# A fused cross-attention and mixture-of-experts kernel: TensorE does the shared chunk ahead of the attention work in steps 16 and later

## The chip, the cores and the metric

The kernel runs on one core of a Trainium2 chip. Its metric is the device time of one execution in microseconds (us). A core has five engines that run their own instruction streams and meet only at semaphores: TensorE (PE: matmuls and transposes), VectorE (DVE), ScalarE (ACT: activation functions and copies), GpSimd (POOL) and SyncE (SP: it issues DMA transfers). Each engine takes its instructions strictly in the order in which they are written, so an instruction that waits holds up all that stand behind it on its engine. PE writes its results to PSUM, from where ACT or DVE take them.

## What is computed

`x` has 4 x 512 rows of 256 numbers, `ctx` has 4 x 64 rows. In float32:

```python
x = x + attn(layernorm(x), ctx)          # 16 heads of 16, softmax over 64 context rows, output product Wo, bias bo
z = layernorm(x)                         # 2048 rows
sh = gelu(z @ sw1[s] + sb1[s])           # s = 0, 1: two shared experts, hidden width 512
shared = (sum_s sh @ sw2[s] + sb2[s]) / 2
gates = z @ router_w + router_b          # 8 experts, the best 2 of each row, softmax over the two
moe = sum over the two chosen experts e of p_e * (gelu(z @ w1[e] + b1[e]) @ w2[e] + b2[e])
out = x + shared + moe
```

## The kernel before

The 2048 rows are 16 tiles of 128 (`NT = 16`). A first part runs attention tile by tile, a second the shared experts, a third the routed experts over rows gathered by expert. Products of the second and third part are split into a high and a low part (`s_hi`, `s_lo`, `xt_hi`, `xt_lo`, `h_hi`, `h_lo`) and summed from three matmuls each.

The first two parts are one pipeline over steps `s = 0 .. 47`, written out on every engine as a loop `for s in range(FIRST_CHUNK + CHUNKS)` with `FIRST_CHUNK = 16` and `CHUNKS = 32`. What a step holds is fixed by hand. On PE (L1146 to L1242), in this order:

- `scores(s + 1)` while there are tiles;
- the **attention part** of the step, four pieces that belong to four tiles: transposes of the normalised rows of tile s - 8 (L1154, `psA<-ident,rows`; two tiles in step 22), the output product of tile s - 4 (L1165, `psD<-WoT,OT`), the values product of tile s - 3 (L1177, `psA<-PT,Vbd`), and the eight transposes of the probabilities of tile s - 2 (L1190, `psP<-ident,Pr`). In steps 16 to 22 this pipeline drains: the last probabilities are transposed in step 17, the last values product is in step 18, the last output product in step 19, the last rows in step 22;
- `queries`, in odd steps up to 11;
- from step 16 on the **shared chunk** `n = s - 16`: in chunk 1 first `gate_rows_out(0)` (L1106, `psS<-ident,gT`), from chunk 2 on `shared_out(n - 2)` (12 matmuls, L1122 and L1125), then six matmuls of the hidden layer (L1215, `psS<-xt_hi,s_lo` and so on);
- after it, in some steps, router work: `gate_cols(0)` in step 16 and `gate_cols(1)` in step 23 (L1098), and the ranking matmuls in steps 19 and 26 (L1237, L1239).

ACT's step (L590 to L648) is not touched: copy of the transposed rows out of psA (L595), copy of the values product into `OT` (L602), normalised rows of tile s - 7 (L610), copy of the transposed probabilities psP into `PT` (L616), and behind these, from step 16 on, the two Gelus of chunk n (L632 into `h_hi`, L633 into `g`). In step 16 a table load (L622) stands ahead of the Gelus, since all activations before it used other functions, and the copy of the gate columns (L637, `gT<-psS`) behind them. DVE's step: residual add of tile s - 4 (L906, `xres<-psD,xres`), statistics, then `h_lo` of chunk n (L929). Behind `h_lo` stand in step 17 `choose(0)` (L785 and L789: it reads the gate rows from PSUM and signals `gates_read`), in step 18 `indices(0)` and `one_hot(0)` (L796 to L808, `ohs`), in step 20 `place(0)`.

Waits of PE that the prediction speaks of: chunk 0 waits for `xlo_done` (DVE L765); `gate_rows_out(0)` waits for `gt_sb` (ACT L637); `shared_out(0)` waits, since it writes the banks from which probabilities and gate rows are read, for `pt_sb` of the last tile (ACT L616) and `gates_read` (DVE L785); the ranking in step 19 waits for `ohs_ready` (DVE L808) and for `x1_done` of the last tile (DVE L906). Later, DVE L982 waits for scatter-adds of POOL, which begin when all results of the shared experts are stored (POOL L502).

Of the kernel before, what the change touches and what calls it, by code (L numbers as in the profile page):

```python
# [17 lines left out]
NT = TOK // P  # L18
# [12 lines left out]
NPAIR = NT // 2  # L31
# [6 lines left out]
CHUNKS = NG * NSH * HC  # L38
CPG = NSH * HC
FIRST_CHUNK = NT  # L40
# [72 lines left out]
def program(nc, ios, keep, scratch):  # L113
# [4 lines left out]
    with ExitStack() as es:  # L118
# [3 lines left out]
        def sem(name):  # L122
            return es.enter_context(nc.semaphore(name))
# [63 lines left out]
        xbo_done, x1_done, x1s_done, sbh_done = sem("xbo_done"), sem("x1_done"), sem("x1s_done"), sem("sbh_done")  # L187
# [33 lines left out]
        def x2T_at(s):  # L221

            return range(s - 8, NT) if s == NT + 6 else range(max(s - 8, 0), s - 7) if s < NT + 6 else ()
# [18 lines left out]
        def row(t):  # L242

            return rows[t // HALF_T][:, t % HALF_T]
# [790 lines left out]
        def _(pe):  # L1035
# [13 lines left out]
            def queries(p):  # L1049
                if p == 1:  # L1050
                    pe.wait_ge(ld_xT0, 16)
                elif p % 2 == 0:
                    pe.wait_ge(ld_xT[2 * p // TPB], 16)
                pe.wait_ge(qt_sb, p)
                for f in range(C):
                    for c in range(C):
                        last = T.matmul(psD[:, f * D:(f + 1) * D], WqT[:, c, f * P:(f + 1) * P], xTs[:, c, p * QT_TOK:(p + 1) * QT_TOK],
                                        start=(c == 0), stop=(c == C - 1))
                last.then_inc(qt_psum, 1)

            def scores(t):
                b = t // TPB
                pe.wait_ge(qt_sb, t // 2 + 1)
                if b == 0:
                    pe.wait_ge(k0_done, 1)
                else:
                    pe.wait_ge(k_done, HPR)
                if t >= 2:
                    pe.wait_ge(shift_done, t - 1)
                for c in range(C):  # L1070
                    for r in range(RT):
                        own = slice(r * L, (r + 1) * L)
                        last = T.matmul(psS[:, t % 2, r, c * HPR * L:(c + 1) * HPR * L], QT[own, t // 2 % 2, c, t % 2 * P:(t % 2 + 1) * P],  # L1073
                                        Kbd[own, c, b].rearrange("p h k -> p (h k)"), start=True, stop=True)
                last.then_inc(scores_done, 1)
# [26 lines left out]
            def gate_rows_out(h):  # L1102

                pe.wait_ge(gt_sb, h + 1)
                for i in range(HALF_G):
                    last = T.transpose(gate_rows[h][:, i * P:(i + 1) * P], gT[:, HALF_G * h + i], ident[:])  # L1106
                last.then_inc(gates_psum, 1)
# [35 lines left out]
                        last = T.transpose(xt_bank[s % 2][:, first:first + P], xg[:, b + u, c * P:(c + 1) * P], ident[:])  # L1143
                last.then_inc(xt_psum, 1)

            for s in range(FIRST_CHUNK + CHUNKS):  # L1146
                if s + 1 < NT:
                    scores(s + 1)
                for t in x2T_at(s):
                    pe.wait_ge(rows_done, t + 1)  # L1150
                    pe.wait_ge(ot_sb, min(s - 3, NT))
                    first = (t - x2T_at(s)[0]) * D
                    for c in range(C):
                        last = T.transpose(psA[:, first + c * P:first + (c + 1) * P], row(t)[:, c * P:(c + 1) * P], ident[:])  # L1154
                    last.then_inc(x2t_psum, 1)
                if 4 <= s < NT + 4:
                    t = s - 4
                    if t == 0:
                        pe.wait_ge(ld_wo, 16)
                    pe.wait_ge(ot_sb, t + 1)  # L1160
                    pe.wait_ge(qt_sb, min(s // 2 + 2, NPAIR))
                    if t >= 1:
                        pe.wait_ge(x1_done, t)
                    for c in range(C):
                        last = T.matmul(psD[:, 0:D], OT[:, t % 2, c], WoT[:, c], start=(c == 0), stop=(c == C - 1))  # L1165
                    last.then_inc(att_psum, 1)
                if 3 <= s < NT + 3:
                    t = s - 3
                    pe.wait_ge(pt_sb, t + 1)
                    if t == 0:  # L1170
                        pe.wait_ge(v_done, 4)
                    if t >= 5:
                        pe.wait_ge(x2t_sb, t - 4)
                    for c in range(C):
                        for j in range(TPB):
                            own = slice(CT * j, CT * (j + 1))
                            last = T.matmul(psA[own, D + c * P:D + (c + 1) * P], Vbd[:, t // TPB, c * P + CT * j:c * P + CT * (j + 1)],  # L1177
                                            PT[:, t % 2, 4 * (j // 2) + 2 * c + j % 2], start=True, stop=True)
                    last.then_inc(ot_psum, 1)
                if 2 <= s < NT + 2:  # L1180
                    t = s - 2
                    pe.wait_ge(probs_done, t + 1)
                    if t == 0:
                        pe.wait_ge(consts, 2)
                        pe.wait_ge(v_done, 4)
                        pe.wait_ge(k_done, HPR)
                    else:
                        pe.wait_ge(pt_sb, t)
                    for j in range(NJ):
                        last = T.transpose(psP[:, j // 4, j % 4 * P:(j % 4 + 1) * P], Pr[:, t % NPR, 2 * j:2 * j + 2].rearrange("p h k -> p (h k)"), ident[:])  # L1190
                    last.then_inc(pt_psum, 1)
                if s % 2 == 1 and 2 <= (s + 3) // 2 < NPAIR:
                    if s >= 4:
                        pe.wait_ge(x1_done, s - 3)
                    queries((s + 3) // 2)

                n = s - FIRST_CHUNK
                if n == 1:
                    gate_rows_out(0)
                if 0 <= n - 2 < CHUNKS - 2:  # L1200
                    shared_out(n - 2)
                if 0 <= n < CHUNKS:
                    q, e, k = n // CPG, n % CPG // HC, n % HC
                    if n == 0:
                        pe.wait_ge(shift_done, NT - 1)
                        pe.wait_ge(s_lo_done, NSH * PPE)
                    if n % CPG == 0:
                        pe.wait_ge(xlo_done, q + 1)
                    if n >= 2:
                        pe.wait_ge(g_done, n - 1)  # L1210
                    i = 0
                    for c in range(C):
                        wc = slice(c * HF + k * P, c * HF + (k + 1) * P)
                        for a, b in ((s_lo, xt_hi), (s_hi, xt_lo), (s_hi, xt_hi)):
                            last = T.matmul(h_bank[n % 2], a[:, e, wc], b[:, q % 2, c], start=(i == 0), stop=(i == 3 * C - 1))  # L1215
                            i += 1
                    last.then_inc(h_psum, 1)
                if n == 0:
                    pe.wait_ge(ld_small, 16 * 4)
                    pe.wait_ge(shift_done, NT)  # L1220
                    gate_cols(0)
                if n == 7:
                    pe.wait_ge(x1_done, NT)
                    pe.wait_ge(slots_ready, 1)
                    gate_cols(1)
                if n == 8:
                    gate_rows_out(1)
                if n in (3, 10):
                    h = n // 10
                    pe.wait_ge(ohs_ready, h + 1)  # L1230
                    pe.wait_ge(consts, 24)
                    if h == 0:
                        pe.wait_ge(x1_done, NT)
                    end = HALF_T if h == 0 else NT + 1
                    for t in range((h + 1) * HALF_T):
                        first = max(t, h * HALF_T)
                        T.matmul(psD[:, first * NE:end * NE].rearrange("p (t e) -> p t e", e=NE), ones[:],  # L1237
                                 ohs[:, t].unsqueeze(1).to_broadcast([P, end - first, NE]), start=(t == 0), stop=False)
                    T.matmul(psD[:, h * HALF_T * NE:(h + 1) * HALF_T * NE], tri[:], ohs[:, h * HALF_T:(h + 1) * HALF_T].rearrange("p t e -> p (t e)"),  # L1239
                             start=False, stop=True).then_inc(ranks_psum, 1)  # L1240
                if CHUNKS - 3 <= n < CHUNKS - 1:
                    x_transpose(n - CHUNKS + 3)  # L1242
# [41 lines left out]
            for t in range(SLOTS + 1):  # L1284
# [26 lines left out]
                if 1 <= t <= SINGLES:  # L1311
                    n = t - 1
# [8 lines left out]
                if 2 <= t < SINGLES + 2:  # L1321
                    n = t - 2
# [129 lines left out]
```

## Time and profile before

| | us |
|---|---|
| median of 3 runs | 349.05 |
| lowest and highest | 346.09, 352.20 |
| the profiled execution | 349.37 |
| its span, first to last instruction | 347.7 |

| engine | busy us | share of the span |
|---|---|---|
| PE | 313.0 | 90% |
| DVE | 227.3 | 65% |
| ACT | 216.8 | 62% |
| POOL | 193.4 | 56% |

Busy time of PE is of matmuls that overlap, and their ends are modelled: the time from one start to the next tells what one takes, and the last of a group seems to run on beside the first of the next. The mean granted TensorE clock is 0.972 of full speed. Steps 16 to 23 lie at about 95 to 131 us in this execution.

### The profile page before, as it was taken

To read this page: it belongs to the slowest core of one execution; us is meant where nothing else is said; L and a number is where in the kernel's file an instruction comes from. 1 tells how busy PE (TensorE), PEld (TensorE's weight loads), DVE (VectorE), ACT (ScalarE), POOL (GpSimd) and SP (SyncE) were. 2 spreads that over 40 slices of the span, in tenths; PEclk is the share of its full clock that TensorE was granted. 3 is DMA by queue.
4 is the path that set the end of the run, shared out by engine and by line. 5 is a ranking of instruction groups with operands and counts; after the bars stand their busy time and mean duration, and the time that the engine had idled before them with its cause. 6 is when DMAs were issued, how large, how long until landed. Compare 5 with 4: busy or idle time off the path is not lost. (4 is left out here: it accounts for less than half of the span.)

```text
span 347.7 us, 7628 instructions
## 1 busy us (share of the span) xinstructions
PE 313.0 (90%) x2366; PEld 273.2 (79%) x2366; DVE 227.3 (65%) x474; ACT 216.8 (62%) x437; POOL 193.4 (56%) x235
## 2 busy tenths in 40 slices
PE   3996998999689999998999999999699999999980
PEld 2764776676467878897898998999599999999980
DVE  0579897898943567787566455667557767666630
ACT  1253675876775786574556656677277777868640
POOL 5446899879893268776460000333456557456563
PEclk9996999999999999999899999999899999999996
DMA  7980000007100472346666523545436557534344
GB/s 248 407 333 2 1 2 1 2 0 270 35 16 3 141 268 79 137 139 178 183 221 182 132 111 105 91 69 93 61 54 86 92 79 109 83 38 50 46 45 45
DMA packets 27910, 36.85 MB, mean 106 GB/s; under 512 B 8384, under 2 KB 22080, under 8 KB 27488
## 3 DMA queue, kind: packets, MB, share of 16 engines
q1 hardware_dynamic: 19984, 25.02, 23.6%
q0 software_dynamic: 7456, 10.04, 17.1%
q10 hardware_dynamic: 432, 1.31, 1.1%
q8 instruction: 20, 0.33, 0.4%
q14 instruction: 18, 0.15, 0.2%
HBM read 23.17 MB, written 13.19 MB: 105 GB/s over the span
## 5 line engine op out<-in xcount | busy, mean ns | idle before, releaser
L508 POOL DMA_INDIRECT out<-xres,meta x39 | 65.1, 1669 | 43.0 <-DMA out<-xres,meta 21.4
L929 DVE TENSOR_TENSOR h_lo<-g,h_hi 128x512 fp32r<-128x512 f32 x32 | 23.3, 728 | 39.8 <-ACT g L633 36.5
L632 ACT ACTIVATE h_hi<-psS,sb1T 128x512 fp32r<-128x512 f32 x32 | 22.0, 688 | 34.5 <-PE psS L1215 30.4
L471 POOL TENSOR_TENSOR Pr<-Pr,inv 128x1024 f32<-128x1024 f32 x16 | 31.3, 1958 | 12.0 <-DVE inv L918 11.9
L718 ACT ACTIVATE s_hi<-psS,b1c 128x256 fp32r<-128x256 f32 x60 | 25.6, 490 | 19.6 <-PE psS L1260 19.6
L1276 PE MATMUL psP<-w_lo,s_hi 128*128 x120 | 30.2, 284 | 3.3 <-DVE xres L982 3.3
L1026 DVE TENSOR_TENSOR s_lo<-sraw,s_hi 128x512 fp32r<-128x512 f32 x30 | 20.6, 688 | 18.7 <-ACT sraw L721 14.8
L1276 PE MATMUL psP<-w_hi,s_hi 128*128 x120 | 30.1, 282 | 0.0
L1215 PE MATMUL psS<-xt_hi,s_lo 128*128 128x512 f32 x64 | 25.9, 405 | 0.0
L721 ACT ACTIVATE sraw<-psS,b1c 128x256 f32<-128x256 f32 x60 | 25.9, 503 | 0.0
L1215 PE MATMUL psS<-xt_lo,s_hi 128*128 128x512 f32 x64 | 25.7, 402 | 0.0
L1276 PEld LDWEIGHTS psP<-w_lo,s_hi 128*128 128x128 f32 x120 | 22.8, 190 | 3.5 <-DVE xres L982 3.5
L1215 PE MATMUL psS<-xt_hi,s_hi 128*128 128x512 f32 x64 | 25.4, 397 | 0.0
L1190 PE MATMUL psP<-ident,Pr 128*128 128x128 f32 x128 | 18.7, 292 | 6.2 <-POOL Pr L471 6.1
L1276 PEld LDWEIGHTS psP<-w_hi,s_hi 128*128 128x128 f32 x120 | 23.0, 192 | 0.0
L1190 PEld LDWEIGHTS psP<-ident,Pr 128*128 128x128 f32 x128 | 14.7, 148 | 10.1 <-POOL Pr L471 8.5
L441 POOL DMA_INDIRECT xg_d<-rows_a,slots x16 | 18.3, 1142 | 7.4 <-issue 4.0
L778 DVE TENSOR_TENSOR w_lo<-wraw,w_hi 128x512 fp32r<-128x512 f32 x32 | 21.9, 714 | 0.0
L633 ACT ACTIVATE g<-psS,sb1T 128x512 f32<-128x512 f32 x32 | 21.8, 682 | 0.0
L441 POOL DMA_INDIRECT xg_d<-rows_b,slots x16 | 18.2, 1137 | 5.3 <-issue 5.1
L886 DVE TENSOR_REDUCE mx<-psS 128x16 f32<-128x1024 f32 x16 | 18.7, 1169 | 3.6 <-PE psS L1073 3.6
L607 ACT ACTIVATE Pr<-Pr,rs 128x1024 f32<-128x1024 f32 x16 | 18.3, 1144 | 4.4 <-DVE Pr L895 4.4
(238 smaller groups left out, 1013.8 us busy)
## 6 DMA issues: line engine op xcount, KB each, us to landing
wraw<-in_w SPq DMA_DIRECT2D x16, 512.0 KB, 5.1
xg<-xg_d SPq DMA_DIRECT2D x15, 256.0 KB
sraw<-in_sw SPq DMA_DIRECT2D x2, 1024.0 KB, 11.3
out<-xres SPq DMA_DIRECT2D x4, 512.0 KB
xres<-in_x SPq DMA_DIRECT2D x3, 512.0 KB, 9.3
xTs<-in_xT SPq DMA_DIRECT2D x3, 512.0 KB, 10.0
xg<-xg_d SPq DMA_DIRECT2D x9, 128.0 KB
xg_d<-filler SPq DMA_DIRECT2D x8, 130.0 KB
```

The costliest lines, as they stand in the source:

```text
L441: pool.indirect_dma_start(xg_d, bass.IndirectOffsetOnAxis(ap=slots[:, k, t:t + 1], axis=0), row(t), None).then_inc(scattered[t // HALF_T][ ...
L471: pool.tensor_tensor(out=Pr[:, t % NPR], in0=Pr[:, t % NPR], in1=inv[:, t % 2].unsqueeze(2).to_broadcast([P, NH, L]), op=ALU.mult).then_in ...
L508: pool.indirect_dma_start(out, bass.IndirectOffsetOnAxis(ap=meta[:, n, 0:1].bitcast(U32), axis=0), y[:, n % NYB], None, compute_op=ALU.add ...
L632: A.activation(h_hi[:, n % 2], h_bank[n % 2], ACT.Gelu, bias=bias).then_inc(hhi_done, 1)
L633: A.activation(g[:, n % 2], h_bank[n % 2], ACT.Gelu, bias=bias).then_inc(g_done, 1)
L718: ins = A.activation(hp_hi[:, i % 2, k], hp_bank[i % 2][k], ACT.Gelu, bias=b1c[:, i % 2, k:k + 1])
L721: ins = A.activation(gp[:, i % 2, k], hp_bank[i % 2][k], ACT.Gelu, bias=b1c[:, i % 2, k:k + 1])
L778: V.tensor_tensor(out=w_cols(w_lo[:, e], k), in0=w_cols(wraw[e], k), in1=w_cols(w_hi[:, e], k).bitcast(F32), op=ALU.subtract).then_inc(lo_ ...
L929: V.tensor_tensor(out=h_lo[:, n % 2], in0=g[:, n % 2], in1=h_hi[:, n % 2].bitcast(F32), op=ALU.subtract).then_inc(hlo_done, 1)
L1190: last = T.transpose(psP[:, j // 4, j % 4 * P:(j % 4 + 1) * P], Pr[:, t % NPR, 2 * j:2 * j + 2].rearrange("p h k -> p (h k)"), ident[:])
L1215: last = T.matmul(h_bank[n % 2], a[:, e, wc], b[:, q % 2, c], start=(i == 0), stop=(i == 3 * C - 1))
L1276: T.matmul(res_bank[n % 2], hp_hi[:, i % 2, c, own], b[:, bass.ds(e, 1), C * HF + c * D:C * HF + (c + 1) * D].squeeze(1), start=(c == 0 an ...
```

## The change

The attention part of a step and the shared chunk become functions, `attention(s)` and `chunk(n)`. Up to step 15 nothing changes. From step 16 on PE does `chunk(s - 16)` first and `attention(s)` after it. No instruction is added or removed, and DVE, ACT, POOL and SP keep their order.

```diff
--- before.py
+++ after.py
@@ -1143,9 +1143,7 @@
                         last = T.transpose(xt_bank[s % 2][:, first:first + P], xg[:, b + u, c * P:(c + 1) * P], ident[:])
                 last.then_inc(xt_psum, 1)
 
-            for s in range(FIRST_CHUNK + CHUNKS):
-                if s + 1 < NT:
-                    scores(s + 1)
+            def attention(s):
                 for t in x2T_at(s):
                     pe.wait_ge(rows_done, t + 1)
                     pe.wait_ge(ot_sb, min(s - 3, NT))
@@ -1189,12 +1187,8 @@
                     for j in range(NJ):
                         last = T.transpose(psP[:, j // 4, j % 4 * P:(j % 4 + 1) * P], Pr[:, t % NPR, 2 * j:2 * j + 2].rearrange("p h k -> p (h k)"), ident[:])
                     last.then_inc(pt_psum, 1)
-                if s % 2 == 1 and 2 <= (s + 3) // 2 < NPAIR:
-                    if s >= 4:
-                        pe.wait_ge(x1_done, s - 3)
-                    queries((s + 3) // 2)
-
-                n = s - FIRST_CHUNK
+
+            def chunk(n):
                 if n == 1:
                     gate_rows_out(0)
                 if 0 <= n - 2 < CHUNKS - 2:
@@ -1215,6 +1209,21 @@
                             last = T.matmul(h_bank[n % 2], a[:, e, wc], b[:, q % 2, c], start=(i == 0), stop=(i == 3 * C - 1))
                             i += 1
                     last.then_inc(h_psum, 1)
+
+            for s in range(FIRST_CHUNK + CHUNKS):
+                if s + 1 < NT:
+                    scores(s + 1)
+                if s < NT:
+                    attention(s)
+                if s % 2 == 1 and 2 <= (s + 3) // 2 < NPAIR:
+                    if s >= 4:
+                        pe.wait_ge(x1_done, s - 3)
+                    queries((s + 3) // 2)
+
+                n = s - FIRST_CHUNK
+                if n >= 0:
+                    chunk(n)
+                    attention(s)
                 if n == 0:
                     pe.wait_ge(ld_small, 16 * 4)
                     pe.wait_ge(shift_done, NT)
```

In the lists below a row is a group of equal matmuls of PE in program order; line numbers are those of each kernel (L1209, L1188, L1175, L1163, L1152 in the changed one are L1215, L1190, L1177, L1165, L1154 before). The first place is the end of step 16 and the start of step 17. Before:

```order
L1215 MATMUL psS<-xt_hi,s_hi 128x512
L1098 MATMUL psS<-x2T_a,rws 32x128 x16
L1154 MATMUL psA<-ident,rows_b 128x128 x2
L1165 MATMUL psD<-WoT,OT 128x256 x2
L1177 MATMUL psA<-PT,Vbd 32x128 x8
L1190 MATMUL psP<-ident,Pr 128x128 x8
L1106 MATMUL psS<-ident,gT 128x128 x2
L1215 MATMUL psS<-xt_hi,s_lo 128x512
L1215 MATMUL psS<-xt_lo,s_hi 128x512
L1215 MATMUL psS<-xt_hi,s_hi 128x512
```

After the change:

```order
L1152 MATMUL psA<-ident,rows_b 128x128 x2
L1163 MATMUL psD<-WoT,OT 128x256 x2
L1175 MATMUL psA<-PT,Vbd 32x128 x8
L1188 MATMUL psP<-ident,Pr 128x128 x8
L1098 MATMUL psS<-x2T_a,rws 32x128 x16
L1106 MATMUL psS<-ident,gT 128x128 x2
L1209 MATMUL psS<-xt_hi,s_lo 128x512
L1209 MATMUL psS<-xt_lo,s_hi 128x512
L1209 MATMUL psS<-xt_hi,s_hi 128x512
L1209 MATMUL psS<-xt_hi,s_lo 128x512
```

`gate_rows_out(0)` (L1106) and the first hidden matmuls of chunk 1 now follow directly on `gate_cols(0)` (L1098). The four attention groups that stood between them have moved behind chunk 1.

The second place is the end of step 17 and the start of step 18, up to the first matmul of `shared_out(0)` (L1122). Before:

```order
L1215 MATMUL psS<-xt_hi,s_hi 128x512
L1154 MATMUL psA<-ident,rows_b 128x128 x2
L1165 MATMUL psD<-WoT,OT 128x256 x2
L1177 MATMUL psA<-PT,Vbd 32x128 x8
L1122 MATMUL psS<-s_lo,h_hi 128x256
```

After the change:

```order
L1209 MATMUL psS<-xt_hi,s_hi 128x512
L1152 MATMUL psA<-ident,rows_b 128x128 x2
L1163 MATMUL psD<-WoT,OT 128x256 x2
L1175 MATMUL psA<-PT,Vbd 32x128 x8
L1188 MATMUL psP<-ident,Pr 128x128 x8
L1122 MATMUL psS<-s_lo,h_hi 128x256
```

Between the end of chunk 1 and `shared_out(0)` stood three groups of step 18; now the four groups of step 17 stand there, and the last of them is the transposes of the last probabilities. Those of step 18 follow behind chunk 2. In steps 19 to 22 the same exchange is made with the rest of the attention part.

## Rows read from the trace of the kernel before

**Rows 1.** Busy us per engine in a stretch; at the end TensorE clock, DMA share, GB/s.
```profile
101.00:106.00 5.00, 4.21 (x52) 3.25 (x41) 2.39 (x4) 4.01 (x9) 2.73 (x3) 1.00 0.08 26
...
124.00:130.00 6.00, 6.00 (x42) 5.21 (x46) 4.08 (x6) 4.80 (x9) 5.20 (x5) 1.00 0.64 236
```

**Rows 2.** Timeline of PE, step 16: start, length, engine, line, operation [idle before].
```profile
95.76 0.44 PE L1154 MATMUL psA<-ident,rows_b 128*128 128x128 f32 x2 [1.00 <-ACT rows_b L610]
...
98.71 0.47 PE L1215 MATMUL psS<-xt_hi,s_lo 128*128 128x512 f32 x1
...
100.27 1.08 PE L1098 MATMUL psS<-x2T_a,rws 128*32 128x128 f32 x32
...
101.28 0.44 PE L1154 MATMUL psA<-ident,rows_b 128*128 128x128 f32 x2
```

**Rows 3.** Timelines of DVE (first row) and ACT (the rest), steps 15 and 16.
```profile
94.89 1.16 DVE L765 TENSOR_TENSOR xt_lo<-x2T_a,xt_hi 128x1024 fp32r<-128x1024 f32 x1
...
98.99 1.03 ACT L616 ACTIVATE PT<-psP 128x1024 f32<-128x1024 f32 x1 [0.38 <-PE psP L1190]
...
100.03 1.28 ACT L622 ACT_TABLE_LOAD   x1
...
102.58 0.38 ACT L637 ACTIVATE gT<-psS 128x256 f32<-128x256 f32 x1
```

**Rows 4.** Timeline of PE, steps 17 and 18.
```profile
103.38 0.65 PE L1177 MATMUL psA<-PT,Vbd 128*32 128x128 f32 x16 [0.79 <-ACT x2T_b L595]
...
103.95 1.09 PE L1190 MATMUL psP<-ident,Pr 128*128 128x128 f32 x8
...
104.88 0.38 PE L1106 MATMUL psS<-ident,gT 128*128 128x128 f32 x2
...
109.09 0.36 PE L1122 MATMUL psS<-s_lo,h_hi 128*128 128x256 f32 x1
...
111.98 0.38 PE L1154 MATMUL psA<-ident,rows_b 128*128 128x128 f32 x2
```

**Rows 5.** Timelines of ACT (first two rows) and DVE (last two), step 17.
```profile
105.08 1.03 ACT L616 ACTIVATE PT<-psP 128x1024 f32<-128x1024 f32 x1
...
106.71 0.69 ACT L632 ACTIVATE h_hi<-psS,sb1T 128x512 fp32r<-128x512 f32 x1 [0.60 <-PE psS L1215]
...
108.00 0.69 DVE L929 TENSOR_TENSOR h_lo<-g,h_hi 128x512 fp32r<-128x512 f32 x1 [2.86 <-ACT g L633]
...
108.61 0.22 DVE L785 TENSOR_TENSOR gates<-psS,rb_bc 128x64 f32<-128x64 f32 x1
```

**Rows 6.** Timelines of ACT (two rows), DVE (two), PE (two), steps 18 to 23.
```profile
109.09 0.39 ACT L602 ACTIVATE OT<-psA 128x256 f32<-128x256 f32 x1 [0.84 <-PE psA L1177]
...
109.37 0.59 ACT L610 ACTIVATE rows_b<-xres,nmr,rs 128x256 f32<-128x256 f32 x1
...
113.48 0.69 DVE L929 TENSOR_TENSOR h_lo<-g,h_hi 128x512 fp32r<-128x512 f32 x1 [2.97 <-ACT g L633]
...
116.24 0.39 DVE L906 TENSOR_TENSOR xres<-psD,xres 128x256 f32<-128x256 f32 x1
...
116.77 0.35 PE L1237 MATMUL psD<-ohs,ones 128*128 128x64 bf16 x8 [0.72 <-DVE xres L906]
...
129.90 1.08 PE L1098 MATMUL psD<-x2T_b,rws 128*32 128x128 f32 x32
```

**Rows 7.** PE after its longest idle times, and the stretches around the last two.
```profile
28.91 1.97 PE L1190 MATMUL psP<-ident,Pr 128*128 128x128 f32 x8 [3.70 <-POOL Pr L471]
...
163.32 0.35 PE L1122 MATMUL psS<-s_lo,h_hi 128*128 128x256 f32 x1 [1.67 <-issue]
...
249.36 0.39 PE L1276 MATMUL psP<-w_lo,s_hi 128*128 x1 [3.29 <-DVE xres L982]
...
160.00:170.00 10.00, 8.33 (x42) 7.03 (x41) 5.13 (x10) 4.11 (x7) 2.94 (x5) 0.83 0.80 231
...
240.00:260.00 20.00, 16.71 (x126) 16.32 (x125) 10.79 (x19) 11.76 (x32) 8.56 (x7) 0.91 0.38 58
```

## The prediction

> **What bounds the kernel now.** I read the stretches first. From 124 us on PE is busy without a break and the clock is full; in 101 to 106 us it is busy for 4.21 of 5 us only [rows 1]. So PE sets the pace, and in steps 16 to 19 it stands still at times for others. What moves the end of these steps moves everything behind them: the shared chunks that follow keep PE full. Next I read PE's timeline there for what it waits on. In step 16 it is idle 1.00 us for the rows [rows 2]. In step 17 it is idle 0.79 us for ACT's copy of the rows [rows 4], in step 19 0.72 us for DVE's L906 [rows 6]. `gate_rows_out(0)` at 104.88 does not wait: the gate columns it needs left ACT at 102.58 + 0.38 = 102.96 [rows 3]. `shared_out(0)` at 109.09 hardly waits: DVE's L785 ends at 108.61 + 0.22 = 108.83 [rows 5]. Both points were covered by attention work of PE, and this is what the change takes away.
>
> **The change, part by part.** No work is added; what counts is who waits for whom. Lengths of PE's pieces, from start to start: an attention part of step 17 is 104.88 - 101.28 = 3.60 us, less 0.79 of idle time and some 0.2 by which the last modelled matmul outlasts its place: 2.6 us, of which the transposes of probabilities take 104.88 - 103.95 = 0.93 [rows 2, 4]. `gate_cols(0)` is 101.28 - 100.27 = 1.0 [rows 2]. `shared_out` and the six hidden matmuls are 111.98 - 109.09 = 2.9 together [rows 4], the hidden ones alone 1.5 (98.71 to 100.27) [rows 2]; in chunk 1 there are the two gate transposes beside them, 1.6. From the end of a DVE instruction to PE's start I count 0.14 us (116.24 + 0.39 to 116.77) [rows 6].
>
> *Step 16.* Chunk 0 must wait for `xt_lo`, which DVE has at 94.89 + 1.16 = 96.05 [rows 3]: it starts at 96.2, later than the rows allowed before (95.76). It is done at 97.7, the attention part at 100.3, `gate_cols(0)` at 101.3: as before. But the transposes of tile 14's probabilities end at 100.4 instead of 98.95, so ACT's copy of them starts at 100.5 instead of 98.99, and behind it on ACT stand the table load, both Gelus and the gate columns [rows 3]. All of these move by 1.5. The gate columns are there at 102.96 + 1.5 + 0.14 = 104.6. PE comes to `gate_rows_out(0)` at 101.3 already, since the attention part of step 17 stands behind it now. **First wait: 3.3 us.**
>
> *Step 17.* Gate rows and chunk 1 run from 104.6 to 106.2, much as before; the attention part from 106.2 to 108.8, and its last transpose ends at 109.0. ACT copies these probabilities at 109.0 (105.08 before). The Gelus of chunk 1 stand behind that copy, at 109.9; before they waited for the chunk until 106.71. `h_lo` comes 108.00 - 106.71 = 1.3 later, the gates 0.6 after that and take 0.2 [rows 5]: 112.1. With 0.14 `shared_out(0)` starts at 112.2 instead of 109.09. PE had finished at 108.8. **Second wait: 3.4 us.**
>
> *Steps 18 and 19.* `shared_out(0)` and chunk 2 take 2.9, the attention part without probabilities 2.6 - 0.93 = 1.7: the last values product is done at 116.8. Behind it on ACT: the copy into `OT` at 116.9, the rows 0.3 later, the Gelus 0.5 after that [rows 6], `h_lo` 1.3 later at 119.0. Then DVE's index work in its old length, from `h_lo` to L906 116.24 - 113.48 = 2.8, and 0.5 from there to the ranking matmuls [rows 6]: 122.2 instead of 116.77, 5.5 late. PE's own work ends at 116.8 + 2.9 + 1.1 = 120.7. **Third wait: 1.5 us.**
>
> *Steps 20 to 23.* `shared_out(n)` of chunk n + 2 needs Gelus that are two steps old. ACT now does rows and copies of a step after the chunk's matmuls, so that the Gelus come about 1.4 later after their chunk, and a step has 2.9 us of shared work: hidden. The rows wait for nothing any more, which gives back some 0.3. `gate_cols(1)`, at 129.90 before [rows 6], comes at 135.1: **+5.2 us**. The weights' transfers start when DVE's L906 is through with the last tile, and move with it; POOL's and SP's work hangs on results that move too. I give nothing back for them.
>
> *The clock.* After idle times of 1.67 and 3.29 us PE's clock fell to 1.2 GHz for a while. The stretches around them show 0.83 over 10 us and 0.91 over 20 us, so 1.7 and 1.8 us lost; after 3.70 us idle the eight transposes took 1.97 [rows 7] against 1.09 [rows 4]. Idle times of 0.79 to 1.00 left the clock at 1.00 [rows 1, 2]. The first new wait of 3.3 us belongs to the first kind, and every matmul from it to the second wait lies on the path: 1.7. So does the second, but what is slow after 116.8 is covered by the third wait: 1.1. Bounds: nothing, if the clock doesn't fall; and at the upper end all 4.2 and 4.6 us of work behind the two waits at half speed, 8.8. I take 2.8, since both measured falls cost less than 2.
>
> Sum: 349.4 + 5.2 + 2.8 = 357.4 against the profiled execution. That one is 0.3 above the median of the runs shown, so **357.0 us**, 2.3% more.
>
> One price on this path is disputed. ACT's table load takes 1.28 us [rows 3], and what stands ahead of it ends at 98.99 + 1.03 = 100.02, just before it starts at 100.03. The Trainium skill (ScalarE: Activation LUTs, What ACT_TABLE_LOAD costs) adds a drain of 1.38 us to each switch of the table set, 2.66 us in all. By that the first wait would be 4.7 and the sum 358.8; the trace shows no such gap here, and I stay with its row.
>
> **The rivals.**
> - *The clock stays full.* For it: each wait lies between stretches of full work, and the fall after 1.67 us idle came only later, with PE busy again. Against it: all three idle times over 1.6 us have slow matmuls behind them [rows 7]. Then 5.2 alone: 354.3 us. Chance 0.24.
> - *The clock stays low over most of the stretch between the waits.* For it: the 1.97 us after 3.70 us idle, and that here two long waits follow each other within 5 us, which the trace has nowhere. It costs 5 instead of 2.8, some 359.5 us. Chance 0.14.
> - *A later wait takes the loss up.* PE is idle for 3.29 us at 249.36 for DVE's L982 [rows 7], with 1.8 lost by the clock. If what ends that wait didn't move, 8.0 - 3.3 - 1.8 leave 2.9: 352 us. Against it: L982 waits for scatter-adds, and their first waits for the stores of all shared results, which are late by the same amount. Chance 0.05.
> - *Faster.* The idle times of 1.00, 0.79 and 0.72 us in PE [rows 2, 4, 6] go, since rows and copies are ready when PE comes to them, and with nothing else that gives 349.0 - 2.5 = 346.5 us. It is decided at `gate_rows_out(0)`: the gate columns would have to leave ACT by 101.2 us, but in the old order already they leave it at 102.96 [rows 3], and the change can only delay them. Chance 0.03.
> - My forecast, both waits and a fall of the clock behind them: the remaining 0.54.
>
> **How the numbers follow.** About 2% can be told from no change here; 2% over 349.05 is 356.0 us. The forecast's own range is 355.5 to 359, about 0.06 of its 0.54 below 356. So slower: 0.48 + 0.14 = 0.62; within 2%: 0.24 + 0.05 + 0.06 = 0.35; faster: 0.03. The range runs from 353.0, just under a clock that stays full, to 361.0, into the case in which it stays low; outside are the two lowest cases and the end of the highest.
>
> **What the profile would show.** PE idle about 3.3 us before L1106, its releaser ACT's gate columns, which leave ACT about 1.5 us later after chunk 0's start than the old order would have them; idle about 3.4 us before the first L1122, released by DVE's gates; about 1.5 us before L1237. Stretches behind the first two with a clock below 1.00. `gate_cols(1)` 5 to 8 us later than at 129.90, and from there to the end the same 218 us. The prediction is wrong if the first two waits are below 2 us, if the clock stays at 1.00 (then 354), or if the idle time ahead of the first scattered results (249.36 now) has shrunk.

## The result and the profile after

| | before | changed |
|---|---|---|
| median (lowest, highest) of 6 runs, us | 348.15 (346.09, 356.03) | 354.66 (352.08, 355.77) |
| ratio, 95% interval | | 1.0192 (1.0150 to 1.0234) |
| profiled execution, us (span) | 349.37 (347.7) | 352.16 (350.4) |
| medians of both again, beside each other on one chip (section on e9; 23 and 6 runs) | 345.04 | 354.44 |
| ratio there, 95% interval | | 1.0256 (1.0221 to 1.0292) |

The changed kernel is slower by 1.9% in the first measurement, whose interval holds 2%, and by 2.6% in the second, whose interval lies above it. The forecast was 357.0 us, 2.3%. Executions more than 1.5% above the fastest of their kernel (352.20 and 356.03 us of the kernel before here, 367.11 in e6) count as slow, and the ratios are made of the others.

PE of the changed kernel, steps 16 to 23 (timeline: start, length, engine, line, operation, idle time before and its releaser; L1209 and L1246 were L1215 and L1237):

```profile
94.71 0.47 PE L1209 MATMUL psS<-xt_hi,s_lo 128*128 128x512 f32 x1 [1.43 <-DVE xt_lo L765]
...
98.94 1.08 PE L1098 MATMUL psS<-x2T_a,rws 128*32 128x128 f32 x32
103.07 0.44 PE L1106 MATMUL psS<-ident,gT 128*128 128x128 f32 x2 [3.05 <-ACT gT L637]
...
110.91 0.36 PE L1122 MATMUL psS<-s_lo,h_hi 128*128 128x256 f32 x1 [3.33 <-DVE gates L785]
...
122.60 0.35 PE L1246 MATMUL psD<-ohs,ones 128*128 128x64 bf16 x8 [1.32 <-DVE xres L906]
...
135.15 1.08 PE L1098 MATMUL psD<-x2T_b,rws 128*32 128x128 f32 x32
```

ACT in steps 16 and 17, then DVE in step 17:

```profile
99.05 1.02 ACT L616 ACTIVATE PT<-psP 128x1024 f32<-128x1024 f32 x1
100.09 1.28 ACT L622 ACT_TABLE_LOAD   x1
...
102.63 0.38 ACT L637 ACTIVATE gT<-psS 128x256 f32<-128x256 f32 x1
...
107.61 1.02 ACT L616 ACTIVATE PT<-psP 128x1024 f32<-128x1024 f32 x1
108.53 0.68 ACT L632 ACTIVATE h_hi<-psS,sb1T 128x512 fp32r<-128x512 f32 x1
```

```profile
109.83 0.69 DVE L929 TENSOR_TENSOR h_lo<-g,h_hi 128x512 fp32r<-128x512 f32 x1 [2.92 <-ACT g L633]
110.44 0.22 DVE L785 TENSOR_TENSOR gates<-psS,rb_bc 128x64 f32<-128x64 f32 x1
```

The stretches of the changed kernel (busy us of PE, PEld, DVE, ACT, POOL; then the clock):

```profile
106.00:112.00 6.00, 2.67 (x32) 2.26 (x33) 2.51 (x13) 3.05 (x5) 0.35 (x2) 0.98 0.02 4
112.00:118.00 6.00, 6.00 (x41) 4.83 (x40) 0.85 (x2) 1.14 (x3) 2.28 (x4) 0.74 0.00 0
...
160.00:170.00 10.00, 9.67 (x61) 8.43 (x60) 9.20 (x27) 5.35 (x9) 8.73 (x5) 1.00 0.53 144
```

Against [rows 2, 4, 6] three idle times stand out: 3.05 us before the gate rows, 3.33 before the first `shared_out`, 1.32 before the ranking. The first is ended by ACT's copy `gT`, which stands behind the copy of the probabilities (99.05), the table load (100.09) and two Gelus. The second is ended by DVE's gates (110.44), behind `h_lo` (109.83), behind Gelus that begin only when ACT has copied the last probabilities (107.61 to 108.53). In 106 to 112 us PE is busy for 2.67 of 6 us. The clock, still at 0.98 there, is at 0.74 in the stretch behind the second wait.

All times below are counted from PE's transposes of tile 13's probabilities, in step 15, since this point itself lay anywhere between 91.5 and 94.1 us in the traces, whatever the kernel. The **local stretch** runs from there to `gate_cols(1)` in step 23: 129.90 - 93.67 = 36.23 us before, 135.15 - 92.19 = 42.96 after.

| from tile 13's transposes, us | before | changed | later by |
|---|---|---|---|
| `gate_cols(0)` | 6.60 | 6.75 | 0.15 |
| gate rows, L1106 | 11.21 | 10.88 | -0.33 |
| first `shared_out`, L1122 | 15.42 | 18.72 | 3.30 |
| ranking, L1237 | 23.10 | 30.41 | 7.31 |
| `gate_cols(1)` | 36.23 | 42.96 | 6.73 |

So the stretch is 6.7 us longer, yet the two profiled executions differ by 2.8 us only. Of the rest, 1.5 us is the earlier point in time of tile 13, and some 2.3 us lie in the kernel before (69.60 against 67.26 us in the section on e1): its first trace had the stall at 163.32 with the clock's fall behind it [rows 7], and the changed kernel's clock was at 1.00 through 160 to 170 us. Whether the change had removed that stall was the first thing to settle.

### The profile page after: what moved, and what is told of

It is laid out like the page before. It is cut to its first block and busy times, and to the rows that moved or that the text cites. A ratio compares the mean times of both kernels' runs of the same rounds, so it can differ in the third digit from the quotient of the medians.

```text
span 350.4 us, 7628 instructions
## 1 busy us (share of the span) xinstructions
PE 311.8 (89%) x2366; PEld 272.7 (78%) x2366; DVE 226.3 (65%) x474; ACT 216.8 (62%) x437; POOL 199.0 (57%) x235
## 3 DMA queue, kind: packets, MB, share of 16 engines
q10 hardware_dynamic: 432, 1.31, 1.1%
## 5 line engine op out<-in xcount | busy, mean ns | idle before, releaser
L929 DVE TENSOR_TENSOR h_lo<-g,h_hi 128x512 fp32r<-128x512 f32 x32 | 23.6, 737 | 36.2 <-ACT g L633 31.6
L1209 PE MATMUL psS<-xt_hi,s_lo 128*128 128x512 f32 x64 | 25.9, 405 | 1.4 <-DVE xt_lo L765 1.4
L1209 PE MATMUL psS<-xt_lo,s_hi 128*128 128x512 f32 x64 | 25.7, 402 | 0.0
L1209 PE MATMUL psS<-xt_hi,s_hi 128*128 128x512 f32 x64 | 25.3, 395 | 0.0
L441 POOL DMA_INDIRECT xg_d<-rows_b,slots x16 | 22.2, 1389 | 5.3 <-issue 5.1
L1188 PE MATMUL psP<-ident,Pr 128*128 128x128 f32 x128 | 18.5, 290 | 6.0 <-POOL Pr L471 5.9
L1188 PEld LDWEIGHTS psP<-ident,Pr 128*128 128x128 f32 x128 | 14.6, 147 | 9.8 <-POOL Pr L471 8.1
L1122 PE MATMUL psS<-s_lo,h_hi 128*128 128x256 f32 x64 | 17.8, 300 | 4.4 <-DVE gates L785 3.3
```

What stands on the lines that cost most here:

```text
L441: pool.indirect_dma_start(xg_d, bass.IndirectOffsetOnAxis(ap=slots[:, k, t:t + 1], axis=0), row(t), None).then_inc(scattered[t // HALF_T][ ...
L929: V.tensor_tensor(out=h_lo[:, n % 2], in0=g[:, n % 2], in1=h_hi[:, n % 2].bitcast(F32), op=ALU.subtract).then_inc(hlo_done, 1)
```

## The experiments

### e1: the kernel before, again

No edit.

> The kernel before, once more, to see what its trace repeats. I measure the local stretch on PE from the transposes of tile 13's probabilities (93.67 in the first trace) to gate_cols(1) (129.90): 36.2 us, and expect 36.0 to 36.5 again. Open is the rest of the span: the first trace had an idle time of 1.67 us of PE at 163 us with a fall of the clock behind it (some 3.4 us in all), which the changed kernel's trace does not have. If this belongs to the kernel before, it stands here too, and the change gives it back; if it comes and goes from run to run, the spans and clocks of the single runs spread by 2 to 4 us.

Measured: 345.56 us against 345.05 for the same kernel (ratio 1.0016, interval 0.9998 to 1.0034). The stretch is 36.23 us again, and each point of the table above agrees within 0.01. Where the stall was (columns as above):

```profile
160.00:165.00 5.00, 5.00 (x33) 4.59 (x34) 2.53 (x6) 2.70 (x5) 2.54 (x3) 1.00 0.86 170
```

PE is busy throughout at full clock. From `gate_cols(1)` to the weight load of the first transposes of gathered rows, 66.71 us pass here, 69.60 in the first trace of before, and 67.26 in the changed kernel's. The stall at 163 us is thus an accident of that execution and not a cost that the change takes away.

### e2, e3, e4: one part of the exchange at a time

The order in the loop is chosen by the step:

```diff
                 if n >= 0:
-                    chunk(n)
-                    attention(s)
+                    if s == 16:                # e3: s == 17, e4: s >= 18
+                        chunk(n)
+                        attention(s)
+                    else:
+                        attention(s)
+                        chunk(n)
```

> Chunk first in step 16 alone, the old order from step 17 on. Theory (the chain through ACT): the gate columns leave ACT 1.5 us late, and so does the copy of tile 9's rows behind them, for which the values product of step 17 waits; its idle time grows from 0.79 to 2.3 us, and the stretch becomes 36.2 + 1.5 = 37.7. Rival (each exchange costs the wait that was seen at its place): 3.1 to 3.3 more, 39.4. Clock stays at 1.00 in the stretch.

> Chunk first in step 17 alone. Theory: PE waits 1.8 us for the gate columns (they leave ACT at their old time), does the transposes of the last probabilities 2.6 us later, ACT's Gelus of chunk 1 move to behind their copy, and the first shared_out starts 1.6 us late; stretch 37.8. Rival (the wait of 3.4 us in front of shared_out belongs to this step alone): 39.6.

> Old order in steps 16 and 17, chunk first from step 18 on. Theory: shared_out(0) waits some 2.4 us for the gates, since it comes when chunk 1 is done and not after three attention groups; the last values product is 2.3 us late and with it the ranking; steps 19 to 22 cost nothing; stretch 36.2 + 2.0 = 38.2. Together with 1.5 and 1.6 of the other two parts this makes 5.1 of the 5.2 us forecast for the whole. Rival (the exchanges from 19 on cost or gain too): a stretch outside 37.7 to 38.7.

| | stretch, us | ratio (interval) |
|---|---|---|
| e2, step 16 only | 37.76 | 1.0085 (1.0051 to 1.0119) |
| e3, step 17 only | 38.00 | 1.0055 (1.0030 to 1.0079) |
| e4, from step 18 | 39.66 | 1.0133 (1.0101 to 1.0165) |

PE's idle times, of e2, e3 and e4 in this order:

```profile
103.63 0.65 PE L1175 MATMUL psA<-PT,Vbd 128*32 128x128 f32 x16 [2.18 <-ACT x2T_b L595]
```

```profile
102.44 0.44 PE L1106 MATMUL psS<-ident,gT 128*128 128x128 f32 x2 [1.65 <-ACT gT L637]
...
109.58 0.64 PE L1175 MATMUL psA<-PT,Vbd 128*32 128x128 f32 x16 [1.37 <-ACT x2T_b L595]
```

```profile
107.73 0.36 PE L1122 MATMUL psS<-s_lo,h_hi 128*128 128x256 f32 x1 [2.42 <-DVE gates L785]
```

e2 and e3 came out as forecast (37.7 and 37.8), and against the rivals at 39.4 and 39.6. The exchange in step 16 costs 1.5 us, of which 1.4 is the wait for ACT's rows, grown from 0.79 to 2.18; that in step 17 costs 1.8. By its medians e2 is 2.5 us longer than the kernel before beside it (347.56 against 345.05), more than its stretch explains; in its trace another 1.0 us lies behind the wait near 250 us, which the end of the part on why the prediction was right takes up. In e4 the stretch is 1.5 us over the forecast of 38.2. Its wait of 2.42 before `shared_out` is the one forecast (2.4). The difference is the clock:

```profile
108.00:110.00 2.00, 2.00 (x13) 2.00 (x13) 0.34 (x4) 0.00 (x0) 1.39 (x5) 0.63 0.04 8
110.00:112.00 2.00, 2.00 (x6) 1.52 (x6) 0.00 (x0) 0.00 (x0) 1.23 (x2) 0.52 0.00 0
```

It falls behind that wait, to 0.63 and 0.52 in four us: 2 x 0.37 + 2 x 0.48 = 1.7 us of PE's work. Without it e4 has 38.0. The three parts make 1.5 + 1.8 + 1.7 = 5.0 us without the clock, against 5.2 forecast for the whole.

### e12: chunk first from step 19 on

As above with `s >= 19`.

> Old order up to step 18, chunk first from step 19 on. Theory (the exchange in steps 19 to 22 costs nothing, since Gelus are needed two steps later and rows are ready): the ranking starts at its old time within 0.3 us, the stretch is 36.0 to 36.3, no fall of the clock, ratio 1.000. Rival (it is part of the loss): 37 or more.

Measured: stretch 35.49, below the 36.0 to 36.3 expected; ratio 1.0005 (0.9986 to 1.0023). PE's timeline at the ranking of step 19:

```profile
116.93 0.35 PE L1250 MATMUL psD<-ohs,ones 128*128 128x64 bf16 x8 [0.72 <-DVE xres L906]
```

From `gate_cols(0)` to the ranking e12 takes 116.93 - 100.44 = 16.49 us, as e1 does. From the ranking to `gate_cols(1)`, at 129.49, it takes 12.56 instead of 129.90 - 116.77 = 13.13 [rows 6]: the exchange in steps 20 to 22 gains 0.57 us. (The rest of the difference in the stretch, 0.16, lies before step 17: here, and in e11, the clock fell already around the start of the stretch, behind idle times of 1.00 and 0.92 us, and the transposes of tile 13 took 1.97 us instead of 1.09.) Its timeline at tile 13:

```profile
92.99 1.08 PE L1175 MATMUL psA<-PT,Vbd 128*32 128x128 f32 x16 [0.92 <-ACT x2T_a L595]
94.00 1.97 PE L1188 MATMUL psP<-ident,Pr 128*128 128x128 f32 x8
```

The gain doesn't show in the time. The waits of PE behind the stretch, of e1 first and of e12 below it, say why (engine, line, waited for: total, times, longest):

```profile
PE psD L1237 <- DVE ohs L808: 0.4, 1, 0.4
```

```profile
PE psD L1250 <- DVE ohs L808: 0.9, 1, 0.9
```

PE now comes earlier to the second ranking, in step 26, and waits for DVE 0.9 instead of 0.4 us there. The whole gain goes there.

### e9: the changed kernel, again

No edit.

> The changed kernel once more, beside the kernel before on the same chip. The waits of the stretch should repeat to 0.1 us (first L1106 10.9 and first L1122 18.7 us after tile 13's transposes); what should vary is where the clock falls: one fall in the first trace. The stretch is 43.0 with one fall, 44 to 45.5 with two or a long one, 41.4 with none. From gate_cols(1) to the first transposes of gathered rows I expect 66.7 to 67.3 us as in five traces so far, not the 69.6 of the very first one of the kernel before; then the ratio is 1.022, a little above the first measurement.

Measured: ratio 1.0256 (1.0221 to 1.0292), above the 1.022 expected. The waits are 3.05, 3.33 and 1.31 us, the gate rows stand at 10.90 (10.88 before), and the stretch is 44.36. Its clock, in two-us stretches behind either wait:

```profile
106.00:108.00 2.00, 2.00 (x6) 1.44 (x5) 0.00 (x0) 0.00 (x0) 0.00 (x0) 0.50 0.00 0
...
116.00:118.00 2.00, 2.00 (x7) 1.69 (x7) 0.00 (x0) 0.00 (x0) 1.63 (x4) 0.50 0.00 0
```

Here the clock fell behind both waits. The first fall delays the first `shared_out` from 18.72 to 20.12, by 1.4 us. The waits of the first trace and of this one are the same, so the same 3.05 us of idle time let the clock fall in one execution and not in the other.

### e5 and e10: PE kept busy in its waits

```diff
                 n = s - FIRST_CHUNK
+                if n in (1, 2):
+                    pe.wait_ge(x1_done, s - 4)
+                    for _ in range(26):        # e10: 13
+                        T.matmul(psD[:, D:D + P], ident[:], ident[:], start=True, stop=True)
                 if n >= 0:
                     chunk(n)
```

The added wait keeps PE out of the bank while DVE reads it; PE shows no idle time at it.

> The changed kernel with 26 matmuls of the identity with itself, whose result nobody reads, in each of its two long waits (ahead of the gate rows in step 17 and ahead of the first shared_out in step 18): 26 x 0.117 = 3.0 us of PE work each. Theory (part of the loss is the clock that falls behind the waits): PE's idle times there shrink to some 0.3 us, the clock stays at 1.00 up to 120 us, the local stretch is 36.2 + 5.2 = 41.4 instead of the 43.0 of the changed kernel's trace, and the runs lie 1 to 2.5 us below the changed kernel's, at a ratio of about 1.013 to before. Rival (the waits alone are the loss, the clock is of no account): the ratio stays at 1.019.

I had mis-sized the filler: the profile shows two records for each float32 matmul, so one takes 0.23 us and not 0.117. The 26 took 5.9 us at each place instead of 3.0, and the kernel's ratio is 1.0581 (1.0544 to 1.0618). The stretch is 46.42, the clock 1.00 all through it. Against the filler of the right size below, the gate rows come 13.70 - 10.91 = 2.79 us too late and the first `shared_out` 23.71 - 18.75 = 4.96, and that is the whole difference to 41.42. As a test of the time it failed. It lost another 10 us behind the stretch, where ACT waits for something whose releaser the profile gives as remote, no engine of the core (ACT's waits of 139 to 220 us; total, times, longest):

```profile
ACT h_hi L632 <- remote: 11.9, 3, 6.4
```

With the right size:

> The changed kernel with 13 instead of 26 filling matmuls of 0.23 us in each of the two long waits, 3.0 us of work each, whose result nobody reads. Theory (part of the loss is the clock): idle times of PE of 0.1 to 0.4 us at both places, clock 1.00 through the stretch, stretch 41.4 to 41.6 instead of 43.0, and runs 1 to 3 us below those of the changed kernel. Rival (clock of no account): stretch 43 and the same time. Whether the 10 us that the version with 26 lost between 150 and 180 us come back is open; if they do, they belong to the longer program of PE and not to the lateness.

Measured: stretch 41.42 us, and 352.70 us where e9, beside it on the same chip, has 354.44; ratio 1.0207 (1.0181 to 1.0233). PE at the first `shared_out`, and the clock behind the two places:

```profile
112.40 0.36 PE L1122 MATMUL psS<-s_lo,h_hi 128*128 128x256 f32 x1 [0.43 <-DVE gates L785]
```

```profile
104.00:106.00 2.00, 2.00 (x14) 1.65 (x13) 0.79 (x2) 0.50 (x2) 0.33 (x1) 1.00 0.00 0
...
114.00:116.00 2.00, 2.00 (x12) 1.64 (x11) 0.00 (x0) 0.30 (x1) 1.82 (x4) 1.00 0.00 0
```

The idle times are 0 and 0.43, the clock doesn't fall, and the gate rows stand at 10.91, the first `shared_out` at 18.75 as in the changed kernel's first trace. This parts the two causes. The waits alone make 41.42 - 36.23 = 5.19 us. The clock makes 1.5 us more in the first trace of the changed kernel, 2.9 in e9, and 1.7 between the medians of e9 and e10 (354.44 and 352.70; their runs overlap only at the edge, 352.56 to 356.83 and 350.93 to 352.99). The 10 us that e5 lost behind the stretch are gone too; since both fillers lengthen the program, and e10's by half as much, I can't say whether length or lateness brought them.

### e6: ACT takes the chunk first too

ACT's two Gelus, with the table load ahead of them, move in front of the copies of the attention part:

```diff
-                for t in x2T_at(s):
...
+                if s == NT:
+                    A.activation(warm[:], half[:], ACT.Gelu)
...
+                    A.activation(h_hi[:, n % 2], h_bank[n % 2], ACT.Gelu, bias=bias).then_inc(hhi_done, 1)
+                    A.activation(g[:, n % 2], h_bank[n % 2], ACT.Gelu, bias=bias).then_inc(g_done, 1)
+                for t in x2T_at(s):
...
-                if s == NT:
-                    A.activation(warm[:], half[:], ACT.Gelu)
...
-                    A.activation(h_hi[:, n % 2], h_bank[n % 2], ACT.Gelu, bias=bias).then_inc(hhi_done, 1)
-                    A.activation(g[:, n % 2], h_bank[n % 2], ACT.Gelu, bias=bias).then_inc(g_done, 1)
```

> The changed kernel with ACT's order exchanged too from step 16 on: the Gelus of the chunk first, then the copies of the attention part, and the copy of the gate columns after them. Theory (the loss comes from ACT's copies standing ahead of its Gelus while PE has them the other way round): both long waits shrink, the first to 0.7, the second to 1.3 us, the ranking starts at its old time, and the stretch is 36.2 again within 0.5. Rival (PE's order alone makes the loss, whatever ACT does): above 40.

Measured: stretch 38.34, ratio 1.0043 (1.0008 to 1.0079). PE's waits:

```profile
95.29 0.47 PE L1210 MATMUL psS<-xt_hi,s_lo 128*128 128x512 f32 x1 [1.45 <-DVE xt_lo L766]
...
98.78 0.64 PE L1176 MATMUL psA<-PT,Vbd 128*32 128x128 f32 x16 [0.78 <-ACT x2T_b L608]
...
101.97 0.44 PE L1107 MATMUL psS<-ident,gT 128*128 128x128 f32 x2 [0.51 <-ACT gT L638]
...
105.50 0.65 PE L1176 MATMUL psA<-PT,Vbd 128*32 128x128 f32 x16 [0.64 <-ACT x2T_b L608]
...
108.38 0.36 PE L1123 MATMUL psS<-s_lo,h_hi 128*128 128x256 f32 x1 [1.21 <-ACT PT L629]
```

The two long waits are 0.51 and 1.21 us as forecast (0.7 and 1.3), so the clash of the two orders is what makes them. But I expected 36.2 and missed by 2.1 us. The rows of the attention part now wait behind Gelus on ACT, and the values products of steps 16, 17 and 18 wait for them, 0.78, 0.64 and 0.64 us (the last at 113.16). With the wait ahead of chunk 0, which the exchange on PE brings, these are 1.45 + 0.78 + 0.51 + 0.64 + 1.21 + 0.64 = 5.2 us of idle time up to the ranking. The old order has 1.00 and 0.79 [rows 2, 4] and two more of 0.18 and 0.64, 2.6 in all. The difference of 2.6 is the ranking's delay, 25.77 against 23.10. The clock is 1.00 all through. So of the 5.2 us by which the changed kernel's stretch is longer without the clock, 3.1 go when ACT's order goes with PE's, and 2.1 remain with the exchange on both engines.

### e7, e8, e11: the table load where ACT idles

```diff
+                if s == NT:
+                    A.activation(warm[:], half[:], ACT.Gelu)
                 if 3 <= s < NT + 3:
                     t = s - 3
                     act.wait_ge(ot_psum, t + 1)
...
                 if s == NT:
-                    A.activation(warm[:], half[:], ACT.Gelu)
                     act.wait_ge(ld_small, 16 * 4)
```

> The changed kernel with ACT's table load for Gelu moved ahead of the copy into OT in step 16, where ACT idles. Theory: the load of 1.28 us leaves the path to the gate columns; the first wait is 1.9 us instead of 3.1 and the stretch, without the clock, 41.4 - 1.3 = 40.1. Rival (a drain of 1.38 us belongs to the switch and lies on the path too): the first wait is shorter by 2.6.

In the changed kernel the wait for the gate rows shrinks from 3.05 to 1.62, by 1.43; the gate rows come 1.41 us earlier. That is the load of 1.28 us and 0.1 of `warm` behind it. ACT at the load, and the clock around the end of PE's second wait (at 109.15), three of the five stretches below full:

```profile
96.25 0.38 ACT L595 ACTIVATE x2T_b<-psA 128x256 f32<-128x256 f32 x1 [1.47 <-PE psA L1153]
96.66 1.28 ACT L598 ACT_TABLE_LOAD   x1
```

```profile
108.00:110.00 2.00, 0.85 (x4) 0.88 (x5) 1.65 (x11) 0.04 (x1) 0.13 (x1) 0.50 0.02 4
...
112.00:114.00 2.00, 2.00 (x7) 1.52 (x6) 0.00 (x0) 0.00 (x0) 0.66 (x1) 0.50 0.00 0
114.00:116.00 2.00, 2.00 (x17) 1.41 (x18) 0.14 (x1) 0.38 (x1) 0.00 (x0) 0.81 0.00 0
```

No gap stands ahead of the load here either (96.25 + 0.38 = 96.63), and the wait did not shrink by 2.6: a drain of 1.38 us, which the Trainium skill (ScalarE: Activation LUTs, What ACT_TABLE_LOAD costs) counts with each switch, is not on this path. The stretch is 42.55 us all the same, since the clock stayed at half for 6.8 us (6 us from 108 us on, and 2 x 0.19 / 0.5 in the last row), twice as long as in e4 (1.7 / 0.5 = 3.4). It fell while PE still waited, so that the first 1.15 us of it cost nothing; the loss is 42.55 - (41.42 - 1.41) = 2.5 us. The ratio is 1.0171 (1.0126 to 1.0215).

> The same move of the table load in the kernel before. Theory: Gelu and the gate columns of chunk 0 come 1.1 us earlier, the copy of tile 9's rows 0.9 earlier, the idle time of 0.79 us in step 17 goes, and everything behind it comes 0.9 earlier: stretch 35.3, ratio 0.997. Rival: the idle times turn up elsewhere (in front of shared_out or the ranking), stretch 36.2.

> The kernel before with the table load moved ahead of the copy into OT in step 16, again, to narrow the interval. Theory: stretch 35.4 as in the first trace, ratio 0.9975. Rival: a gain that later waits give back, ratio 1.000.

In the kernel before the same move gives stretches of 35.38 and 35.21 (0.16 of the latter lies ahead of step 17), as forecast; the idle time of 0.79 us in step 17 is gone. The ratios are 0.9982 (0.9951 to 1.0014) and 0.9987 (0.9966 to 1.0008). So it gains 0.9 us in the stretch, and whether a quarter of a percent reaches the end isn't settled by these runs. No version here beats the kernel before by more than that.

## Why the prediction was right

The time lay in the range and on the forecast side, and the mechanism was the one named: PE runs ahead of ACT and waits. The steps of the sum can be held against the traces one by one; the size of the clock's part and the reference were off.

- **First wait, 3.3 us forecast, 3.05 measured** (3.1 from start to start: 103.07 - 98.94, less `gate_cols(0)`'s 1.0). Its place, its releaser and its length hold. e2 and e7 show its two links: the gate columns follow ACT's copy of tile 14's probabilities, and the table load lies on the path with 1.28 us and nothing more.
- **Chunk 0 waits for `xt_lo`, forecast to start at 96.2.** It starts 94.71 - 92.19 = 2.52 us after tile 13's transposes, on the clock of before at 96.19. `gate_cols(0)`, forecast as before, is 0.15 later.
- **Second wait, 3.4 forecast, 3.33 measured.** `shared_out(0)` came 3.30 us late, forecast 3.1.
- **Third wait, 1.5 forecast, 1.32 measured.** The ranking without any fall of the clock stands in e10 at 28.87, 5.8 us late; forecast 5.5.
- **Steps 20 to 23 give back 0.3: measured 0.57** (e12). The mechanism was right; the size was half.
- **Lateness of `gate_cols(1)` without the clock, 5.2 forecast, 5.19 measured** (e10). That it is so close is luck: the small errors above cancel.
- **The claim that nothing behind the stretch answers was slightly wrong.** The second ranking waits 0.9 instead of 0.4 us, 0.5 us more, and takes back what steps 20 to 22 gained. From `gate_cols(1)` to the end the first trace of the changed kernel has 215.3 us and e10 216.2; the kernel before has 214.8 in e1, and the 218 of the prediction held the stall.
- **The clock, 2.8 forecast: 1.5 and 2.9 in two traces, 1.7 between medians (e10 against e9).** This was the mis-sized term. I took a fall behind the first wait as certain, at 1.7. It came in e9, at 1.4, and not in the first trace, with the same wait. For the fall behind the second wait I took 1.1, because the third wait would cover a part: it cost 1.5 at the ranking in both traces (30.41 - 28.87 in the first), since it was over before the third wait, which stayed at 1.3. The prediction also said that idle times of 0.79 to 1.00 leave the clock at 1.00; e11 and e12 show a fall behind two such idle times. The rival of a clock that stays low over most of the stretch between the waits, for 5 us, which I gave 0.14, was seen in no trace; e7 has one long fall, but behind the second wait and for 2.5.
- **The rival of a later wait that takes the loss up fell.** PE idles for 3.27 us at 252.23 in the changed kernel too, where it had 3.29 at 249.36 [rows 7]; the wait moved with the work ahead of it.
- **The rival "faster" fell** where it was said to be decided: the gate columns left ACT 10.8 us after tile 13's transposes in the changed kernel, while PE was through with `gate_cols(0)` at 6.75 + 1.0 = 7.8.
- **The reference point misled.** I added the loss to 349.4 us, an execution with 2.9 us of accidental stall and slow clock in it (69.60 against 66.71, e1). Three later chips ran the kernel before at medians of 345 to 347 us. With the 345.04 us that stand beside e9 the same loss of 8.0 us gives 353.0 for a kernel that took 354.44. That the forecast in microseconds, 357.0 against 354.66, looks too high and not too low is thus owed to the reference. The ratio, 2.3% forecast against 1.9% and 2.6% measured, is the sounder comparison.

What stays open is how large the rest is. Beside each other on one chip e10 is 352.70 - 345.04 = 7.7 us over the kernel before by the medians, 0.0207 x 345.04 = 7.1 by the ratio (6.2 to 8.0 by its interval). Less 5.19 for the stretch and 0.5 for the second ranking, 1.4 to 2.0 us are left (0.5 to 2.3 by that interval). In the traces a second place differs. Behind the wait near 250 us [rows 7] the same work of PE, from its restart to the next transposes of gathered rows, takes 5.72 us in e1 (244.57 to 250.29) and 6.71 in e10 (252.31 to 259.02), for the clock is below full there for longer (first row e1, the others e10; a part of the 5 us from 250 on lies in the wait):

```profile
245.00:250.00 5.00, 5.00 (x34) 5.00 (x34) 0.00 (x0) 0.89 (x3) 1.55 (x1) 0.75 0.35 34
```

```profile
250.00:255.00 5.00, 2.69 (x12) 2.69 (x13) 2.19 (x4) 0.00 (x0) 2.48 (x2) 0.57 0.23 26
255.00:260.00 5.00, 5.00 (x35) 5.00 (x34) 0.55 (x1) 2.15 (x6) 1.98 (x2) 0.74 0.26 31
```

With the 0.5 of the second ranking these 1.0 us make up the 1.45 us that e10's trace has more than e1's from `gate_cols(1)` to the end. But they are not shown to come from the change. In the fourteen traces the wait there is 3.27 to 3.56 us, and the work behind it takes from 4.40 us (e3, where the clock doesn't fall) to 7.14 (e4); the changed kernel's first trace has 5.67, and e8, in the old order, has 7.09:

```profile
247.69 0.39 PE L1289 MATMUL psP<-w_lo,s_hi 128*128 x1 [3.27 <-DVE xres L982]
...
248.00:250.00 2.00, 2.00 (x19) 2.00 (x18) 0.00 (x0) 0.00 (x0) 0.07 (x1) 1.00 0.61 66
```

(Both rows are of e3.) So the fall at this place goes with the execution, and one trace of each kernel can't say whether the medians' remaining 1.4 to 2.0 us are more than that.

## What to carry to other kernels

Before work is moved on one engine, read what stands behind it on the engines that take its results: here ACT kept its order, and a copy that had been needed first came second, so that each chunk's Gelus queued behind an attention part which PE had just put off. Work that looks like an obstacle ahead of a waiting instruction may be its cover; count what a wait costs once the cover is gone, and then count the clock that may fall behind it. To part the two, fill the wait with idle matmuls of its measured length.

## What the runs showed of the hardware

- The same idle time of 3.05 us of PE, between the same instructions, was followed by a fall of the clock to half in e9 and not in the first trace of the changed kernel. Even the 2.42 us of e4 were followed by one, and in e11 and e12 idle times of 1.00 and 0.92 us, while 3.27 us near 250 us were followed by none in e3. How long it stayed at half varied too, from 3.4 us (0.02 x 6 / 0.5 + 0.26 x 6 / 0.5 in 106 to 118 us of the first trace) to 6.8 us (e7).
- A float32 matmul of 128x128 shows as two records of PE and takes 0.23 us (52 records for the 26 of e5, 5.91 us); the eight transposes of probabilities show as eight records in 0.93 us. Whoever takes the time of one from the transposes, or by records, gets half.
- ACT's table load takes 1.28 us with no gap ahead of it, at all three places where it was put (100.03 us before, 96.66 in e7, 95.72 in e6).
- The filler of the right size moved neither the gate rows nor the first `shared_out`: results of the stretch repeat from trace to trace to 0.03 us when the clock doesn't fall (10.88, 10.90, 10.91 for the gate rows).
